# The next rows of an attention and expert kernel: transposed by VectorE in 32 by 32 blocks and moved into place by DMA, in place of TensorE

## What is computed

```python
# layer 1: cross attention to 77 context rows, 16 heads of 32, then an MLP
q = (LN(x) @ Wq + bq)                       # per token
k, v = ctx @ Wk + bk, ctx @ Wv + bv         # per batch entry, 77 rows
out = softmax(q k^T / sqrt(32)) v           # per head
x = x + relu(out @ W1 + b1) @ W2 + b2       # 512 -> 1024 -> 512
# layer 2: eight experts, each token goes to the one with the largest logit
u = LN(x)
top1 = argmax(u @ Wg.T)
x = x + gelu((LN(u) * s[top1] + c[top1]) @ E1[top1] + e1[top1]) @ E2[top1] + e2[top1]
```

## Time and profile before

| | |
|---|---|
| median of 3 runs | 1403.75 us (1402.22 to 1404.26) |
| the profiled execution | 1402.3 us, its span 1400.3 us |
| TensorE busy, granted clock | 99% of the span, 0.999 |
| VectorE, ScalarE, GpSimd busy | 71%, 44%, 24% |
| DMA | 118 MB in 56916 packets, 84 GB/s on the mean |

### The profile page before, as it was taken

One profiled execution on the slowest core, in us unless ns is written; L12 is line 12 of the kernel. 1 busy time (PEld: TensorE's weight loads), 2 busy tenths in 40 slices (PEclk: granted clock), 3 DMA queues, 4 the chain that ended last, 5 costly groups with the idle time before them and its releaser, 6 DMA issues.

```text
span 1400.3 us, 23958 instructions
## 1 busy us (share of the span) xinstructions
PE 1382.0 (99%) x8590; PEld 1039.6 (74%) x8590; DVE 991.0 (71%) x2073; ACT 612.0 (44%) x1146; POOL 334.0 (24%) x293
## 2 busy tenths in 40 slices
PE   8999999999999999999999999999999999999998
PEld 5486868677776868686867777686868686788897
DVE  6667676686767676777767676767676766649887
ACT  4534334443424343534434342524243343448886
POOL 2311212021111212121201111121212120108887
PEclk9999999999999999999999999999999999999999
DMA  7200302021120303130212102020202021458885
GB/s 293 75 30 1 91 1 77 31 88 46 40 89 24 104 3 99 36 98 31 84 46 68 61 31 84 6 91 1 91 1 91 1 61 61 158 182 266 295 261 178
DMA packets 56916, 118.16 MB, mean 84 GB/s; under 512 B 8329, under 2 KB 16786, under 8 KB 55906
## 3 DMA queue, kind: packets, MB, share of 16 engines
q1 hardware_dynamic: 46002, 82.93, 19.2%
q0 software_dynamic: 10800, 33.70, 6.3%
HBM read 73.77 MB, written 44.66 MB: 85 GB/s over the span
## 4 chain that ended last, share of the span: by engine, by line
PE 96%; DVE 2%; issue 1%; POOL 1%; DMA 0%; ACT 0%; POOLq 0%; SPq 0%; DVEq 0%; ACTq 0%
PE bank L1176 25%; PE bank L1220 13%; PE bank L1200 12%; PE bank L1011 12%; PE bank L1099 8%; PE bank L1081 5%; PE bank L1601 4%; PE bank L1639 3%; PE bank L1036 3%; PE bank L1262 2%; PE bank L979 2%; PE bank L1585 2%; PE bank L1280 1%; PE bank L1055 1%; PE bank L883 1%
## 5 line engine op out<-in xcount | busy, mean ns | idle before, releaser
L1176 PE MATMUL bank<-actA,w 128*128 128x512 f32 x1536 | 368.8, 395 | 1.4 <-DVE actA L1147 1.4
L1176 PEld LDWEIGHTS bank<-actA,w 128*128 128x128 f32 x1536 | 282.4, 188 | 63.5 <-issue 5.6
L1089 ACT ACTIVATE E<-bank 77x512 f32<-77x512 f32 x256 | 132.3, 591 | 170.1 <-PE bank L1081 170.1
L1220 PE MATMUL bank<-w,actH 128*128 128x512 f32 x768 | 195.6, 400 | 0.0
L1200 PE MATMUL bank<-w,actH 128*128 128x512 f32 x768 | 184.8, 393 | 0.0
L1011 PE MATMUL bank<-actA,wq 128*128 128x512 f32 x768 | 182.7, 390 | 0.0
L1049 DVE TENSOR_REDUCE mx<-bank 128x4 f32<-128x308 f32 x256 | 104.6, 472 | 101.1 <-PE bank L1036 101.1
L1220 PEld LDWEIGHTS bank<-w,actH 128*128 128x128 f32 x768 | 138.6, 188 | 44.5 <-issue 18.3
L1011 PEld LDWEIGHTS bank<-actA,wq 128*128 128x128 f32 x768 | 142.7, 188 | 28.2 <-issue 0.5
L1200 PEld LDWEIGHTS bank<-w,actH 128*128 128x128 f32 x768 | 142.0, 188 | 28.2
L1185 ACT ACTIVATE actH<-bank,b 128x512 fp32r<-128x512 f32 x128 | 88.2, 689 | 161.8 <-PE bank L1176 160.2
(11 more groups left out here) (179 smaller groups left out, 1911.1 us busy)
## 6 DMA issues: line engine op xcount, KB each, us to landing
rowB<-region SPq DMA_DIRECT2D x71, 258.0 KB, 3.8
xn<-in_x SPq DMA_DIRECT2D x64, 256.0 KB, 2.8
rows<-in_x SPq DMA_DIRECT2D x64, 256.0 KB, 3.3
w_raw<-in_W SPq DMA_DIRECT2D x2, 2048.0 KB, 11.8
e_raw<-in_E SPq DMA_DIRECT2D x16, 256.0 KB, 2.8
region<-padrow SPq DMA_DIRECT2D x9, 258.0 KB, 4.2
e_parts<-e_high SPq DMA_DIRECT2D x8, 256.0 KB, 2.0
e_parts<-e_low SPq DMA_DIRECT2D x8, 256.0 KB, 2.3
```

The costliest lines, as they stand in the source:

```text
L1089: act.activation(E[0:M, g % 2, h, :], of("ST", b, g, h)[0:M, :], ACT.Exp).then_inc(S["act_exp"], 1)
L1176: mm = pe.matmul(p[:], w, a, start=k == 0 and j == 0, stop=k == KD - 1 and j == 2)
L1220: mm = pe.matmul(p[:], actH[:, ha, m, P * s:P * s + P], w2[:, hw, m, :], start=n == 0, stop=n == 23)
```

## The change

For all blocks but block 0, TensorE no longer transposes the next rows.

1. `XNLOAD` reads rows in another order: tile s holds rows 128 t + 32 s + j of the block on partition 32 t + j.
2. `XSTAT` ends with four instructions on VectorE that transpose each 32x32 block of a tile by itself and put the four tiles side by side in `xq` (128 partitions, 16 feature groups, 4 tiles, 32), which takes the low half of `actQ` once the scores of the block have been made.
3. `XTD`, on SP: 16 DMAs inside SBUF, from 32 partitions of `xq` to 32 partitions of `xn`, runs of 512 bytes, 64 KB each, 1 MB in all. They wait for the four transposes and add to one semaphore.
4. `XTS`: ACT copies `xn[k]` to the high part of `actA` after all 16 have landed, DVE subtracts for the low part.
5. The order: loads are issued ahead of the H stage; in plain blocks `XSTAT` comes before the H stage and `X2STAT` after the transposes, all of it before `OH`; in expert blocks `XSTAT` begins after the first H part. `e1_raw` and `e1_acc` move from `xn` to the bytes of `xq`, so the load of W1 of an expert waits for the last scores, and the transposes wait for its store.

```diff
@@ -106,9 +106,8 @@
     rows = [r[0] for r in rows]
     csb, _ = sb("csb", [P, BLK])
-    xn = [sb(f"xn{i}", [P, D]) for i in range(SUB)]
-    xn_at = xn[0][1]
-    xn = [t[0] for t in xn]
+    xn_all, xn_at = sb("xn", [P, SUB, D])
+    xn = [xn_all[:, i, :] for i in range(SUB)]
     b2bc, _ = sb("b2bc", [P, D])
...
@@ -168,6 +167,10 @@
     w2_raw = at("w2_raw", [P, MF, D], F32, w2_at + 4 * MF * D)
+    xq = at("xq", [P, D // HD, SUB, HD], F32, actQ_at + 4 * KD * BLK)
     e1 = at("e1", [P, KD, NE, EH], F32, wq_at)
...
@@ -206,8 +209,8 @@
     e2_low = at("e2_low", [P, D], F32R, xn_at)
     e2_high = at("e2_high", [P, D], F32R, xn_at + 4 * D)
-    e1_raw = at("e1_raw", [P, KD, EH], F32, xn_at + 8 * D)
-    e1_acc = at("e1_acc", [P, 2, EH], F32, xn_at + 12 * D)
+    e1_raw = at("e1_raw", [P, KD, EH], F32, actQ_at + 4 * KD * BLK)
+    e1_acc = at("e1_acc", [P, 2, EH], F32, actQ_at + 4 * KD * BLK + 4 * KD * EH)
     o[0] = rows_at[0]
...
@@ -387,12 +391,19 @@
                 step("TAB_LOAD")
                 step("EB_LOAD")
+            else:
+                step("XNLOAD", b + 1, 2)
+                step("XNLOAD", b + 1, 0)
             prep = b - 1 - PREP0 if PREP0 < b <= PREP0 + NE else None
             if prep is not None:
                 step("E1_ACC", prep)
+            elif last:
+                step("X2STAT", b - 1)
+                step("DRIP", 8)
             elif b:
-                step("X2STAT", b - 1)
+                step("XSTAT", b + 1)
                 step("DRIP", 8)
...
@@ -415,23 +426,18 @@
                 if b == 0 and m == 6:
                     step("GATE")
-                if prep is not None and m == 1:
-                    step("X2STAT", b - 1)
                 if m:
-                    step("DRIP", 6)
-                if not last and m == 0:
-                    step("XNLOAD", b + 1, 0)
-                if not last and m == 0 and prep is None:
-                    step("XNLOAD", b + 1, 2)
+                    step("DRIP", 6 if b else 8)
                 if context is not None and m == 0:
                     step("VLOAD", context)
-                if not last and m == 3 and prep is not None:
-                    step("XNLOAD", b + 1, 2)
                 if prep is not None and m == 2:
                     step("E1_CENTER", prep)
                     step("E1_STORE", prep)
-                if b and m == 3:
+                if b and m == 3 and prep is None:
                     step("DRAIN")
+                if b and not last and m == (3 if prep is None else 4):
+                    step("XTD", b + 1)
+                    step("X2STAT", b - 1)
                 if b and m == logits + 1:
...
@@ -448,7 +454,7 @@
                     step("EB1_LOAD")
                     step("XLOAD", 1)
-                if m == (3 if prep is None else 4) and not last:
+                if m == 2 and b == 0 or m == 0 and prep is not None:
                     step("XSTAT", b + 1)
...
@@ -474,15 +480,17 @@
                 prep = b - PREP0 if PREP0 <= b < PREP0 + NE else None
                 step("DRAIN")
+                if b == 0:
+                    step("XTD", b + 1)
                 step("YA", b, 0)
                 for s in range(SUB):
                     step("XB", b + 1, s)
                 step("Y", b, 0)
-                for s in range(2):
-                    step("XT", b + 1, s)
+                for k in range(2):
+                    step("XTS", b + 1, k)
                 step("YA", b, 1)
-                for s in range(2, SUB):
-                    step("XT", b + 1, s)
+                for k in range(2, KD):
+                    step("XTS", b + 1, k)
                 if prep is not None:
...
@@ -690,17 +698,21 @@
         def sp_xnload(sp, b, s0):
             for s in (s0, s0 + 1):
+                if b == 1:
+                    sp.wait_ge(S["pe_xT"], s + 1)
+                    sp.wait_ge(st_v, 16 * (NB - 1))
+                elif b:
+                    sp.wait_ge(S["dve_xT"], SUB * b)
+                if PREP0 + 2 <= b < PREP0 + 2 + NE and s0 == 0:
+                    sp.wait_ge(st_e2, 32 * (b - PREP0 - 1))
+                x = A["x"][b * BLK:b * BLK + BLK, :]
                 if b:
-                    sp.wait_ge(S["pe_xT"], SUB * (b - 1) + s + 1)
-                if b == 1:
-                    sp.wait_ge(st_v, 16 * (NB - 1))
-                if PREP0 + 2 <= b < PREP0 + 2 + NE:
-                    if s0:
-                        sp.wait_ge(st_e1, 16 * (b - PREP0 - 1))
-                    else:
-                        sp.wait_ge(st_e2, 32 * (b - PREP0 - 1))
-                sp.dma_start(xn[s][:], A["x"][b * BLK + P * s:b * BLK + P * s + P, :]).then_inc(ld_xn[s], 16)
+                    x = x.rearrange("(t s j) d -> s t j d", s=SUB, j=HD)[s]
+                    sp.dma_start(xn[s], x).then_inc(ld_xn[s], 16)
+                else:
+                    sp.dma_start(xn[s][:], x[P * s:P * s + P]).then_inc(ld_xn[s], 16)
         def sp_xload(sp, b):
...
@@ -720,7 +732,7 @@
         def sp_e1raw(sp, e):
-            sp.wait_ge(S["pe_xT"], SUB * (PREP0 + e + 2))
+            sp.wait_ge(S["pe_s"], KD * (PREP0 + e + 2))
             sp.dma_start(e1_raw[:], A["E1"][:, :, e, :]).then_inc(L["e1raw"], 16)
...
@@ -729,7 +741,7 @@
         def sp_e2raw(sp, e):
-            sp.wait_ge(S["pe_xT"], SUB * (PREP0 + e + 2))
+            sp.wait_ge(S["dve_xT"], SUB * (PREP0 + e + 2))
             sp.dma_start(e2_raw[:], A["E2"][:, e, :]).then_inc(L["e2raw"], 16)
...
@@ -754,7 +766,7 @@
             sp.dma_start(b2e[:], A["Eb2"].to_broadcast([P, NE, D])).then_inc(L["eb"], 16)
         def sp_tabload(sp):
-            sp.wait_ge(S["pe_xT"], SUB * NBLK)
+            sp.wait_ge(S["dve_xT"], SUB * NBLK)
             sp.dma_start(jt[:], A["jt"][:, 0:N1, :]).then_inc(L["jt"], 16)
...
@@ -968,6 +980,15 @@
                                       ALU.subtract, ALU.mult).then_inc(S["dve_xn"], 1)
                     yield
+                if b:
+                    dve.wait_ge(S["pe_s"], KD * b)
+                    if PREP0 + 1 < b <= PREP0 + 1 + NE:
+                        dve.wait_ge(st_e1, 16 * (b - PREP0 - 1))
+                    for s in range(SUB):
+                        dve.wait_ge(S["dve_xn"], SUB * b + s + 1)
+                        dve.transpose(xq[:, :, s, :], xn[s].rearrange("p (n j) -> p n j", j=HD)
+                                      ).then_inc(S["dve_xnT"], 1)
+                        yield
             chains.append(chain())
...
@@ -978,6 +999,29 @@
                 mm = pe.transpose(p[:, P * k:P * k + P], xn[s][:, P * k:P * k + P], ident[:])
             mm.then_inc(S["pe_xT"], 1)
+        NXT = (P // HD) ** 2
+        def sp_xtd(sp, b):
+            sp.wait_ge(S["dve_xnT"], SUB * b)
+            src = xq[:].rearrange("p (k f) s j -> p k f (s j)", k=KD)
+            for t in range(P // HD):
+                for f in range(P // HD):
+                    sp.dma_start(xn_all[HD * f:HD * f + HD, :, P * t:P * t + P], src[HD * t:HD * t + HD, :, f]
+                                 ).then_inc(ld_xT, 16)
+        def act_xts(act, b, k):
+            act.wait_ge(ld_xT, 16 * NXT * b)
+            act.wait_ge(S["pe_h"], MF * b)
+            act.activation(actA[:, 0, k, :], xn_all[:, k, :], ACT.Identity).then_inc(S["act_xT"], 1)
+        def dve_xts(dve, b, k):
+            if k == 0:
+                drain()
+            dve.wait_ge(S["act_xT"], SUB * b + k + 1)
+            dve.tensor_tensor(actA[:, 1, k, :], xn_all[:, k, :], f32(actA[:, 0, k, :]), ALU.subtract
+                              ).then_inc(S["dve_xT"], 1)
         def act_xT(act, b, s):
```

5 lines of the change are left out of this document (4 added, 1 removed).

## The result

The changed kernel takes 1475.51 us, median of 4 runs (1466.16 to 1477.37), where the kernel before, run beside it, takes 1404.01 (1402.22 to 1405.29): ratio 1.051, 95% interval 1.046 to 1.055. It is slower by 5%, 71 us, and outside the range of 1392 to 1421 that was given.

What follows compares the result with a forecast made beforehand. TensorE's stream, 96% of the chain of waits, was taken as the bound. -26.7 + 13.8 + 8.4 + 4.8 = +0.3 on 1402.3 gave 1402.6, as a median 1404; own range 1398 to 1410, overall 1392 to 1421.

Steps and rivals of the forecast that it cites:

- Removed: TensorE's W2 products: without 16 transposes among them, a gain of 1.78 us a block in 15 blocks, 26.7 in all.
- The transpose: VectorE's 32x32 transposes of 128x512: 0.61 us each, four a block, 2.44.
- Plain blocks: Six blocks without expert preparation: one-hot behind normalizations and transposes, a TensorE hole of 2.3 us at the rank products, 13.8 in all.
- Expert blocks up to the first issue: Eight blocks: loads 1.0 us late, 0.3 absorbed, a hole of 0.25 at the rank products, then normalizations and transposes to 534.9.
- Expert blocks after it: Issues, landing, ScalarE's copies and VectorE's subtraction bring Q to 548.0, not 547.65; with the earlier hole 0.6 a block, 4.8 in all.
- The prediction's own sign of being wrong: TensorE's stream: wrong if plain blocks have no rank-product hole, or it waits anywhere else over 1 us a block.
- With the source in SBUF in place of PSUM: nothing: ScalarE's evictions and VectorE's subtractions: they stay, and reading from SBUF costs nothing.
- The scatter of finished rows moves back by some 13 us ... Hidden: Scatter, and behind it row load, W2's read and bias add, come later at no cost until it slips 2 us more.
- Block 0: First block, where VectorE also converts W2: transposes done at 86.2, subtractions at 99.2, a hole of 8.4 us before Q.
- the list of signs: Waits to look for: rank products about 2.3 in six blocks, block 1's first Q about 6, expert blocks both under 0.5.
- hidden by what follows: Block 0's last eviction comes behind the transposes on VectorE, claimed to cost nothing.
- The row loads are the bound: Rival: loads on a quarter of the engines at 103 ns, 13.6 us in expert blocks, not 4.8; 1413; chance 0.16.

Runs made afterwards that it cites:

- six: The change with copies on two queues, handed over in groups, additions after subtractions, loads 32 outermost, one-hot before normalizations and transposes in plain blocks: 1380.45 us, ratio 0.984.
- scat_late: The changed kernel with POOL's scatter, and the row load and bias additions behind it, waiting for VectorE's last subtraction: 1455.6 us, ratio 1.038.
- bias_late: The changed kernel with POOL's four bias additions moved behind VectorE's four subtractions: 1456.8 us, ratio 1.037.
- two_queues: The changed kernel with 11 of the 16 copies issued by SP and 5 by ScalarE's queue: 1407.7 us, ratio 1.0038.
- pieces: The changed kernel with ScalarE's copies and VectorE's subtractions by groups of 128 tokens, each once its own four copies have landed: 1427.4 us, ratio 1.017.

## Why the prediction was wrong

**Removed: right.** 48 W2 products take 10.88 where 12.68 was spent; 1.8 fifteen times.

**The transpose: right.** 0.61 was taken; four take 2.48.

**Plain blocks: right in place, 2.3 a block against 1.73 measured** (10.4 for 13.8). The one-hot behind normalizations and transposes was the cause, as six shows by taking it away. Not foreseen: the lower clock after two of these six waits (1.7 us each).

**Expert blocks up to the first issue: nearly right.** The first copy goes out at t = 22.3 to 24.4, 23.2 in the mean, for 23.1. The one-hot is late by 0.24 in block 6, for 0.25, but that is luck: in the eight blocks it is 0 to 1.69 late, 4.9 us in all for 2.0. The loads ran at a quarter of the engines, as the rule that the prediction cited (the Trainium skill, DMA: Bandwidth & Descriptors, "Why a DMA increments its semaphore by 16 and not by 1") gives it; the trace agrees, 0.26 of the busy share.

**Expert blocks after it: this is the step that failed,** "copies 0.1 + 8.1 + 2.0, ScalarE and VectorE 2.8". It was 12.9 us in all, and is 17.7 in the mean of eight blocks. From the first issue to the start of the last: 10.0 for 8.1 (the median issue takes 602 ns, and from one start to the next it is 0.65 or more, above my upper bound of 0.62). From there to the landing: 3.2 for 2.0; without the scatter and the row load it is 0.6 + 1.46 = 2.1 (scat_late), so the 2.0 was right for a landing alone. Copies and subtractions: 4.5 for 2.8, of which 3.16 is their time alone. That is 4.8 us eight times, 38, and the waits are 37.4. There was no slack in that chain: Q could start at t = 35.8 and the forecast had it ready at 36.1, so each us of error went to the end whole. I gave the sum its ends for the transposes, issues and loads, but none for landing and for the last piece, and I put nothing on all being late together. The prediction's own sign of being wrong, a wait elsewhere of more than 1 us a block, is there: 4.7 us before Q in the mean of the eight.

**"With the source in SBUF in place of PSUM: nothing"** failed. Alone, such subtractions mean 685 ns (bias_late), four in 2.50, which is what they mean from PSUM (681, L991 before); beside POOL's additions four take up to 5.71. The Trainium skill (SBUF — State Buffer, "Who interferes with whom") says just this: a VectorE instruction with two SBUF inputs contends with a GpSimd instruction that reads SBUF, because its second input comes through a read interface that the two engines share, while one with a single SBUF input doesn't (outside VectorE's two-port modes). The trace agrees: L1023 takes 1.4 us each beside POOL and bias_late takes that away, while in the kernel before L991, with one source in PSUM, ran beside the same additions at 0.64 each. POOL's timeline and VectorE's, of the kernel before:

```profile
542.03 5.00 POOL L1001 TENSOR_TENSOR rows<-rows,b2bc 128x512 f32<-128x512 f32 x4 [4.50 <-DVE xn L968]
...
543.49 1.27 DVE L991 TENSOR_TENSOR actA<-bank,actA 128x512 fp32r<-128x512 f32 x2
```

**"The scatter of finished rows moves back by some 13 us ... Hidden"** failed on the side that I did not look at. I asked who waits for it and not what it meets: it now fell on the copies' landing, and so did the first row load behind it, and the bias additions fell on the subtractions. That it stops being hidden for its own users was right, and scat_late walked into it.

**The clock wasn't in the forecast at all.** 17.8 us after the waits before Q, and 7.8 elsewhere: 26 of 65. The prediction treated a wait as costing its own length.

**Block 0: nearly right in its times, 8.4 against 12.9 in its term.** First issue at 86.02 (86.2), Q at 101.23 (99.2). The wait before Q is 8.15 (the sum has 8.4, and the list of signs "about 6", which do not agree). 16 issues took 10.44, the landing 1.46, the rest 3.17; that the last eviction comes late was not "hidden by what follows", it cost 2.02 at L1244. The other 2.7 are lower clock.

```profile
86.02 10.44 SPq L1011 DMA_DIRECT2D xn<-xq  x16
...
97.92 2.19 ACT L1017 ACTIVATE actA<-xn 128x512 fp32r<-128x512 f32 x4 [16.97 <-DMA xn<-xq]
...
98.59 2.50 DVE L1023 TENSOR_TENSOR actA<-xn,actA 128x512 fp32r<-128x512 f32 x4 [9.52 <-ACT actA L1017]
```

These three rows (SP's queue, ScalarE, VectorE) are the cleanest measure of the chain, with nothing beside it.

**The rivals.** "The row loads are the bound" was right in its mechanism and small: between 4 and 14. No rival had the chain behind the copies late, and yet the prediction itself said that it had no room; a rival with the issues at 0.65, the landing at 3.2 and 1.7 us more for copies and subtractions would have given the 38 us (said with the result in hand).

What stays open: why waits of 1.73 were followed by a lower clock in two plain blocks of six and not in the others (in other runs with the same waits, in two to four of six). The four timed runs of the changed kernel span 11 us (a fifth on record, not in the median, took 1480.26), and only the fastest has a profile; that the others differ by longer waits of the same kinds is likely and not shown.

## What to carry to other kernels

When work moves from an engine to DMA, price the whole chain up to its last consumer, and compare its end with the moment at which the bound engine asks: here a chain without slack that was 4.8 us too long in half of the blocks brought 37 us of waits and, with the clock behind them, most of the 5%. Look at what runs beside each step in its new place, on the shared ports and on the DMA engines as on the queues, since a chain 3 us shorter (two_queues) met neither the scatter nor the additions in the expert blocks. Count more than its length for a wait of TensorE (4.7 us cost 6.3 to 7.9 here), and a chain that has to be in time is best shortened by a second queue and by handing over in pieces.

## What the runs showed of the hardware

- Two queues issue side by side: SP's eleven copies took 7.14 us while ScalarE's last four took 2.78. The Trainium skill (DMA: Bandwidth & Descriptors, "Issuing engines are not separate DMA queues") says that a second issuing engine saves only sequencer time, usually small relative to the transfer. The trace agrees on what is saved, and not here on its being small: 16 copies of 64 KB spend 10.4 us in issue and land 1.46 after it.
- A landing is stretched by other queues' traffic: 1.46 us after the last issue alone, 1.8 to 3.3 beside the scatter (and, in expert blocks, the first row load), though the copies alone keep the engines busy for only 0.44 of their time (565 to 571 us of the changed kernel, 104 GB/s).
- VectorE's 32x32 transpose of 128x512 fp32 takes 0.61 to 0.62 us each in a row (four in 2.48), as a bn_stats does (four in 2.46).
- After a wait of 4.26 to 8.15 us before Q, the granted clock was low for several us in every case, and 24 products took 7.0 to 8.6 in place of 5.6; after waits of 1.09 and 1.77 there they took 5.7. In pieces and scat_late waits of 2.2 to 3.1 went either way (7.33 after 2.21, 5.70 after 2.92).
